# Reciprocals of the row sums taken straight to the first pass's outputs, without a product with ones

## The reference, cut to what matters

```python
scores = jnp.where(mask[:, None], scores, -jnp.inf)
attn = jax.nn.softmax(scores, axis=-1)
out = jnp.einsum('bhqk,bhkd->bqhd', attn, v).reshape(b, s, H * VD)
return out @ o_w
```

## Time and profile before

| | |
|---|---|
| device time, median of 3 runs | 897.29 us |
| lowest, highest | 896.67 us, 899.58 us |
| profiled execution, span from first to last instruction | 897.2 us |
| PE busy in the span | 805.0 us, 90% |
| DVE busy | 675.8 us, 75% |
| ACT busy | 596.7 us, 67% |
| POOL busy | 531.0 us, 59% |

### The profile page before, as it was taken

The page is one execution under the profiler, slowest core; times in us unless marked ns, Lnnn a source line. Parts: engine busy times, 40 slices in busy tenths (PEclk is TensorE's granted clock), DMA queues, the critical chain, the costliest instruction groups (busy, mean ns, idle before and its releaser), DMA issues.

```text
span 897.2 us, 20231 instructions
## 1 busy us (share of the span) xinstructions
PE 805.0 (90%) x7496; PEld 500.7 (56%) x7496; DVE 675.8 (75%) x1557; ACT 596.7 (67%) x1340; POOL 531.0 (59%) x440
## 2 busy tenths in 40 slices
PE   4979989977777988898988899999999999999998
PEld 2445544444344655565555567777767777764443
DVE  5365677789998989999999788888888888861000
ACT  2656789978886878787887676776666767750000
POOL 3185368876884555545545587888878788840000
PEclk9989999999998999999999999999999999999999
DMA  8012211112333444443443288788778777880110
GB/s 254 24 36 74 80 41 54 58 31 85 105 114 89 130 125 115 131 111 111 136 129 105 65 137 167 135 137 155 149 147 147 141 137 152 165 168 15 68 51 32
DMA packets 168786, 96.67 MB, mean 108 GB/s; under 512 B 116720, under 2 KB 142704, under 8 KB 168688
## 3 DMA queue, kind: packets, MB, share of 16 engines
q1 hardware_dynamic: 168688, 95.37, 45.8%
HBM read 36.62 MB, written 6.29 MB: 48 GB/s over the span
## 4 chain that ended last, share of the span: by engine, by line
PE 28%; POOL 22%; DVE 21%; issue 15%; DMA 5%; SPq 4%; ACT 4%; POOLq 0%; DVEq 0%; ACTq 0%
PE psS L773 9%; DVE m L1176 5%; DMA arena<-arena 4%; DVE bias L1183 4%; DVE arena L1042 3%; DVE arena L1236 3%; SPq L451 3%; PE psS L700 3%; PE psT L572 2%; PE psT L552 2%; PE psS L529 2%; POOL arena L1356 2%; POOL arena L1469 2%; POOL bias L1422 2%; ACT arena L804 2%
## 5 line engine op out<-in xcount | busy, mean ns | idle before, releaser
L804 ACT ACTIVATE arena<-psT 128x512 f16<-128x512 f32 (+4 forms) x360 | 171.9, 506 | 107.0 <-PE psT L757 67.1
L700 PE MATMUL psS<-keyT,arena 128*128 128x512 f16 (+3 forms) x1152 | 232.6, 330 | 5.2 <-issue 3.0
L1236 DVE CUSTOM_DVE_ANT_0 arena<-psS,bias 128x512 f32<-128x512 f32 (+7 forms) x256 | 191.9, 751 | 36.7 <-PE psS L700 17.0
L991 ACT ACTIVATE arena<-arena,small 128x512 f32<-128x512 f32 (+7 forms) x256 | 197.5, 774 | 31.0 <-DVE small L1236 30.1
L1042 DVE SCALAR_TENSOR_TENSOR arena<-psT,arena 128x512 f16<-128x512 f32 (+3 forms) x278 | 146.1, 545 | 26.3 <-ACT arena L804 25.7
L757 PE MATMUL psT<-ident,arena 128*128 128x128 f32 x736 | 117.3, 281 | 26.3 <-DVE arena L1042 24.3
L700 PEld LDWEIGHTS psS<-keyT,arena 128*128 128x128 f16 x1152 | 92.6, 99 | 57.1 <-issue 8.1
L585 PE MATMUL psS<-ikT,big 128*128 128x512 f16 (+3 forms) x528 | 102.8, 339 | 23.9 <-DVE bias L1127 20.0
L757 PEld LDWEIGHTS psT<-ident,arena 128*128 128x128 f32 x736 | 86.1, 143 | 59.1 <-ACT arena L991 32.3
L1422 POOL TENSOR_TENSOR bias<-arena,bias 128x768 f32<-128x768 f32 (+2 forms) x48 | 91.4, 1918 | 32.7 <-ACT arena L870 22.3
L1183 DVE MATCH_REPLACE8 bias<-m,bias 128x768 f32<-128x768 f32 (+4 forms) x112 | 89.9, 809 | 0.0
(11 more groups left out here) (164 smaller groups left out, 1387.2 us busy)
## 6 DMA issues: line engine op xcount, KB each, us to landing
arena<-arena SPq DMA_DIRECT2D x192, 128.0 KB, 2.4
arena<-in_wiq SPq DMA_DIRECT2D x32, 256.0 KB, 2.7
arena<-in_ow SPq DMA_DIRECT2D x16, 512.0 KB, 3.5
arena<-in_qbT SPq DMA_DIRECT2D x16, 256.0 KB, 2.5
wvo_parts<-arena SPq DMA_DIRECT2D x16, 256.0 KB, 2.0
arena<-in_qpe SPq DMA_DIRECT2D x16, 128.0 KB, 3.0
arena<-in_x SPq DMA_DIRECT2D x8, 256.0 KB, 3.2
out<-arena SPq DMA_DIRECT2D x8, 256.0 KB, 2.0
```

What stands on the lines that cost most here:

```text
L700: last = mm(bank[:, k:k + w], Q[:, u % 2, h, a, q:q + P], keyT[:, b, h, k:k + w], start=(a, b) == (0, 0), stop=(a, b) == (1, 0))
L804: return nc.scalar.activation(dst, src, ACT.Copy, scale=scale)
L991: nc.scalar.activation(pr[:, g % 4, 0:kw], pr[:, g % 4, 0:kw], ACT.Exp, bias=shift[:, g % 4:g % 4 + 1], scale=-1.0, accum_out=rsum[:, unit ...
L1236: v.tensor_tensor_reduce(out=pr[:, g % 4, 0:kw], in0=bank[:, 0:kw], in1=bias[:, TOFF[t]:TOFF[t + 1]], scale=-c_s, scalar=3e38, op0=ALU.add ...
```

## The change

In the first pass the product with the table of ones is left out: the reciprocals go to the output product as they are. The semaphore `ri_done` therefore counts one per unit in the first pass and two in the second, and the table keeps only the second pass's row.

```diff
-        scaled = small[:, 408:424].rearrange("p (c s) -> p c s", c=2)
+        scaled = small[:, 408:416]
...
                 dve.wait_ge(exp_done, 8 * u + 8)
                 v.reciprocal(rinv, rsum[:, u % 2, :]).then_inc(ri_done, 1)
-                dve.wait_ge(ri_done, 2 * u + 1)
-                v.tensor_tensor(rinv, rinv, scaled[:, u // NP], ALU.mult).then_inc(ri_done, 1)
+                if u >= NP:
+                    dve.wait_ge(ri_done, 2 * u - NP + 1)
+                    v.tensor_tensor(rinv, rinv, scaled, ALU.mult).then_inc(ri_done, 1)
                 dve.wait_ge(av_mm, UNIT_AV[u])
-                dve.wait_ge(ri_done, 2 * u + 2)
+                dve.wait_ge(ri_done, u + 1 if u < NP else 2 * u - NP + 2)
                 if u:
                     dve.wait_ge(ot_mm, u)
                 v.tensor_tensor(op.rearrange("p k (h r) -> p h k r", h=2),
...
-            g.memset(small[:, 408:424], 1.0).then_inc(ones_ok, 1)
+            g.memset(scaled, 1.0).then_inc(ones_ok, 1)
             pool.wait_ge(ones_ok, 1)
-            g.memset(scaled[:, 1, 4:8], PR_S).then_inc(eps_ok, 1)
+            g.memset(scaled[:, 4:8], PR_S).then_inc(eps_ok, 1)
```

## The result

The changed kernel takes 888.79 us (median of 5 runs, 887.55 to 889.45) against 897.72 us (median of 5 runs of the kernel before, 896.67 to 899.58): 8.9 us less. The ratio is 0.9897, with a 95% interval of 0.9879 to 0.9915, that is 7.6 to 10.9 us.

What follows compares the result with a forecast made beforehand. The prediction took DVE to bound the first pass, with a loop through PE and ACT next. Its terms, 8.9 - 0.9 + 0.6 = 8.6 us off the 897.2 us span, plus 0.1 us around it, gave 888.7 us, range 885.4 to 893.0.

Steps and rivals of the forecast that it cites:

- the start of the sum: Whole kernel: the time before the change, a span of 897.2 us with 0.1 us around it (median 897.29).
- the gain of 8.6: Whole kernel: the net saving in us, 8.9 - 0.9 + 0.6.
- DVE bounds the first pass; what it is spared shows almost one for one: First pass: DVE works 182.30 of 192.63 us; time it is spared shortens the run until PE or ACT takes over.
- The products cost 8.9 us, not their bare 2.9, because they wait for POOL: First pass, units 0 to 13: products 8.35 us plus hand-overs 0.56 us, as DVE stands until POOL's instruction ends.
- A tenth, 0.9 us, lost to PE and ACT: First pass: in some units a PE transpose or ACT copy comes late instead, taking 0.9 us of the gain.
- Half of 1.2 us from the clock: First pass, units 1 and 5: two slow-clock stretches cost about 1.2 us; 0.6 us is won, bounds 0 and 1.2.
- Nothing for units 14 and 15: Around the start of the second pass: these two products hide behind other waits; uncovered they would give 1.7 us more.
- The second pass moves forward whole: Second pass: a fixed beat of 18.79 us a unit, so an earlier end of the first pass moves it all forward.
- 0.1 us around the span: Whole kernel: measured time exceeds the profiled span by 0.1 us, turning 888.6 into 888.7 us.
- the bare product's 2.9: Rival, first pass: only the unhindered price counts, 2.9 us, up to 5 us, giving 892.2 to 894.3; chance 0.12.
- the rival without gain: First pass: the loop DVE, PE, ACT sets the pace, DVE waits longer for ACT; within 2.7 us of 897.3; chance 0.06.
- the second pass kept its beat: Denies the slower rival: second pass settles in a longer beat, 1 us more giving 902.7 us; chance 0.04.

Runs made afterwards that it cites:

- the constant 1.0: Kernel before, with the first pass's product with the table replaced by a product with the constant 1.0: 898.43 us, 0.9998 of the kernel before.
- the second reciprocal: Kernel before, with the first pass's product replaced by another reciprocal of the same row sums: 891.66 us, 0.9917 of the kernel before.
- the fourth step: Changed kernel, with the unit before finished in step four of the first pass instead of step five: 883.67 us, 0.9846 of the kernel before.

## Why the prediction was right

888.7 us was predicted, 888.79 measured, but the close agreement hides errors that cancel: the start of the sum, 897.29, was 0.4 us under the median of five runs, and the gain of 8.6 was 0.3 us too small. By the prediction's own steps:

- **DVE bounds the first pass; what it is spared shows almost one for one.** Right, and more fully than thought: 8.5 us less busy, 9.6 us less in the 14 units of the two profiles, 8.9 (7.6 to 10.9) by the medians. The run without products in the second pass shows the other side of it.
- **The products cost 8.9 us, not their bare 2.9, because they wait for POOL.** Right in size and cause. Shortening POOL, changing the operation and moving the product each took the stall away or left it as the theory says. The condition in the theory under test, two SBUF inputs, is too narrow: a product with a constant has one, and takes up to 1.21 us too. That POOL must be reading SBUF stays open, since every POOL instruction beside the products did.
- **A tenth, 0.9 us, lost to PE and ACT.** Mis-sized: nothing was lost. The 8.9 us and the 0.7 us of the next point make up the whole 9.6, and PE still waited 14.8 us for DVE afterwards, in 30 places of the 14 units.
- **Half of 1.2 us from the clock.** Near. DVE's idle time in units 1 and 5 fell from 1.50 and 1.38 us to 0.94 and 1.20, 0.7 us together, and no stretch of these 14 units is at half clock (a granted clock of 0.50) any more. The profile with the constant 1.0, whose stalls are as long, has two such stretches; the eight other profiles, with at most one long stall each in these units, have none. That speaks for a tie between the long waits and the clock, but not for one through PE's wait of 2.00 us behind unit 1's product, ahead of the half clock from 326 to 328 us in the earlier trace rows. In the profile with the constant 1.0, PE waits 2.00 us at the same place and its clock stays up behind it; it falls at 395 and 423 us instead, as the lines below this list show. No run changed the clock alone, so none shows the 0.6 us of the sum as such: that half of the 1.2 us would be won was the author's estimate, and the runs show the 0.7 us less of idle time in its place.
- **Nothing for units 14 and 15.** Right for unit 14: the idle time behind it grew by 0.99 us. Unit 15's gave nothing either: the stretch that holds both products took 39.33 us instead of 39.24, with 1.55 us less work on DVE.
- **The second pass moves forward whole.** Right: 18.79 us before and after. The prediction's check on it was weaker than it looked: the reciprocal at 802.5 is unit 31's, and unit 30's, which 801.1 was meant for, comes at 798.28, so the last beat is shorter.
- **0.1 us around the span.** Wrong: 1.8 us. The profiled execution before was one of the longer ones, which put the sum's start near the median by chance, not by the step.

PE in the profile with the constant 1.0, then the windows behind its wait and at 395 us:

```profile
324.75 0.41 PE L757 MATMUL psT<-ident,arena 128*128 128x128 f32 x2 [2.00 <-DVE arena L1042]
...
325.00:329.00 4.00, 3.58 (x39) 2.50 (x38) 3.87 (x11) 3.76 (x11) 0.90 (x1) 1.00 0.28 60
395.00:399.00 4.00, 3.34 (x19) 2.58 (x19) 4.00 (x12) 3.12 (x10) 1.16 (x1) 0.59 0.25 53
```

The rivals all fell with the result: 8.9 us is three times the bare product's 2.9, DVE's wait for ACT over the 14 units stayed at 7.5 us where the rival without gain had some 17, and the second pass kept its beat.

## What to carry to other kernels

A small VectorE instruction isn't cheap because it is small. Look at the spread of its durations, not the median: a minimum of 166 ns and a maximum of 1153 ns on equal shapes say that here it waited for something inside its own time. What ends with it on the timeline is the suspect, and shortening that instruction tells whether it is the cause (here the products then took 0.17 us each). On an engine that sets the pace, such an instruction is best left out, given a form that doesn't stall (the second reciprocal took 0.20 us in the same place), or put where the other engine stands; and an instruction that can move is worth trying right ahead of a place where its engine waits anyway, as in the fourth step here.

## What the runs showed of the hardware

- A reciprocal of 128x8 never stalled on POOL (0.19 to 0.21 us in every kernel), a product with a constant did (0.17 to 1.21 us), and so did a product of two SBUF tiles (0.17 to 1.15 us). The output product of a PSUM bank and an SBUF tile never did (0.69 us).
- The stretches of PE at half clock (a granted clock of 0.50) are 3 to 7 us long in these profiles and don't come at the same places in every execution: the profile before has one around 284 us, from 281.0 to 287.8, and the one after has none there, though up to there the kernels differ only in the table at the start. Of the seven profiles that finish units in the fifth step, the five with this stretch reach the first reciprocal at 305.47 to 306.90 us, the two without it at 304.39 and 304.56. Such stretches go with times that differ by as much as a small change: of 15 runs of the kernel before, one with a mean granted clock of 0.992 took 896.65 us and one with 0.983 took 902.52.
